# First experts: one expert ahead in two banks, or two and four ahead in three

## The reference

```python
logits = x @ router_weight.T
topw, topi = jax.lax.top_k(jax.nn.softmax(logits, axis=-1), 8)
topw = topw / jnp.sum(topw, axis=-1, keepdims=True)
...
gu = jnp.einsum('ech,ehf->ecf', xe, gate_up_proj)   # 64 experts, 128 rows, 256 -> 192
g, u = jnp.split(gu, 2, axis=-1)
h = jax.nn.silu(g) * u
ye = jnp.einsum('eci,eih->ech', h, down_proj)       # 96 -> 256
```

## Time and profile before

| | us |
|---|---|
| median of 3 timed runs | 817.23 (816.66 to 817.79) |
| span of the profiled execution | 851.6 |
| TensorE busy in it | 786.6 (92%) |
| VectorE, ScalarE, GpSimd busy | 556.9, 394.8, 271.2 |
| the expert stage, first to last down product | 433.4 to 547.6 |

### The profile page before, as it was taken

The page is one execution under the profiler, slowest core; times in us unless marked ns, Lnnn a source line. Parts: engine busy times, 40 slices in busy tenths (PEclk is TensorE's granted clock), DMA queues, the critical chain, the costliest instruction groups (busy, mean ns, idle before and its releaser), DMA issues.

```text
span 851.6 us, 16159 instructions
## 1 busy us (share of the span) xinstructions
PE 786.6 (92%) x4635; PEld 660.7 (78%) x4635; DVE 556.9 (65%) x1423; ACT 394.8 (46%) x898; POOL 271.2 (32%) x357
## 2 busy tenths in 40 slices
PE   8998999999899999999879998899999799999957
PEld 7887877778787887777677877788897688888746
DVE  4324778877778787777345555468856387778536
ACT  1334656656565666655123343323333266666411
POOL 2004445534333232222345545524415100000241
PEclk9999999999999999999889999999999999999979
DMA  7449950000000000073176999687621335555321
GB/s 212 102 107 384 406 198 34 34 27 27 21 27 28 20 21 14 27 240 135 51 230 184 323 319 296 213 288 257 246 99 69 106 112 150 149 149 153 95 69 49
DMA packets 62881, 120.74 MB, mean 142 GB/s; under 512 B 18272, under 2 KB 32864, under 8 KB 62688
## 3 DMA queue, kind: packets, MB, share of 16 engines
q1 hardware_dynamic: 51824, 95.41, 35.2%
q0 software_dynamic: 7680, 21.51, 7.0%
q10 hardware_dynamic: 3312, 3.02, 1.0%
HBM read 76.13 MB, written 43.78 MB: 141 GB/s over the span
## 4 chain that ended last, share of the span: by engine, by line
PE 65%; DVE 11%; issue 11%; ACT 4%; POOL 3%; another core or an unknown queue 3%; DMA 2%; DVEq 0%; SPq 0%; ACTq 0%; POOLq 0%
PE scores L1627 9%; PE scores L1625 8%; PE scores L1626 8%; PE scores L1849 5%; PE acc_ps L2035 4%; PE misc_ps L1755 3%; PE probsT_ps L1762 3%; PE probsT_ps L1740 3%; PE misc_ps L1753 3%; DVE xT_lo L1096 3%; PE scores L1859 3%; PE acc_ps L1740 2%; PE probsT_ps L1979 2%; DVE neg_max L1090 2%
## 5 line engine op out<-in xcount | busy, mean ns | idle before, releaser
L826 ACT ACTIVATE area<-scores,neg_max 128x128 f32<-128x128 f32 (+7 forms) x128 | 94.9, 742 | 87.7 <-DVE neg_max L1090 85.5
L1090 DVE TENSOR_REDUCE neg_max<-scores 128x1 f32<-128x128 f32 (+7 forms) x128 | 95.8, 750 | 22.1 <-PE scores L1712 20.8
L708 POOL DMA_INDIRECT xe_d<-x_rows,send_i x64 | 64.1, 1001 | 55.5 <-ACT x_rows L850 38.5
L738 POOL DMA_INDIRECT ye_d<-area,home_i x64 | 61.4, 959 | 58.7 <-issue 28.6
L1849 PE MATMUL scores<-area 128*96 128x128 f32 x512 | 69.1, 279 | 2.1 <-issue 1.3
L1625 PE MATMUL scores<-kT_hi,weff_hi 128*128 128x512 f32 (+3 forms) x172 | 66.8, 388 | 0.9 <-ACT area L803 0.4
L1849 PEld LDWEIGHTS scores<-area 128*96 128x96 f32 x512 | 60.5, 166 | 5.2 <-issue 2.7
L1627 PE MATMUL scores<-kT_hi,weff_lo 128*128 128x512 f32 (+3 forms) x172 | 61.7, 359 | 0.0
L1626 PE MATMUL scores<-kT_lo,weff_hi 128*128 128x512 f32 (+3 forms) x172 | 61.5, 358 | 0.0
L696 POOL CAST weff_hi<-area 128x256 fp32r<-128x256 f32 x42 | 17.0, 406 | 136.5 <-PE scores L1712 88.8
L1755 PE MATMUL misc_ps<-xT_lo,xT_hi 128*128 128x512 f32 x144 | 58.4, 406 | 2.2 <-DVE xT_lo L1096 2.1
(11 more groups left out here) (290 smaller groups left out, 2081.4 us busy)
## 6 DMA issues: line engine op xcount, KB each, us to landing
area<-w SPq DMA_DIRECT2D x23, 512.0 KB, 4.0
area<-gate_up SPq DMA_DIRECT2D x24, 384.0 KB
xe_d<-area SPq DMA_DIRECT2D x8, 1088.0 KB, 11.3
ye_d<-area SPq DMA_DIRECT2D x8, 1024.0 KB, 16.7
area<-w SPq DMA_DIRECT2D x8, 1024.0 KB, 7.2
area<-ye_d SPq DMA_DIRECT2D x15, 512.0 KB, 5.2
area<-xe_d SPq DMA_DIRECT2D x28, 272.0 KB
area<-down SPq DMA_DIRECT2D x24, 192.0 KB
```

The lines of the kernel that those rows point to most:

```text
L826: act.activation(row_of(n)[:, 0:L], score_bank(n)[:, 0:L], ACT.Exp, bias=neg_max[:, n % 4:n % 4 + 1], accum_out=rsum[:, s, k:k + 1]).then_ ...
L1090: dve.tensor_reduce(neg_max[:, n % 4:n % 4 + 1], score_bank(n)[:, 0:(n // HEADS + 1) * P], AX.X, ALU.max, negate=True).then_inc(max_ready, 1)
```

## The change

The buffers `xeT`, `sg` and `hT` become three deep. The banks behind T are now `pT[0]`, `pT[1]` and `acc`, those behind G are `half[0]`, `half[1]` and `misc`; the two banks behind D and the rings of eight stay. TensorE's list becomes T(e+4), G(e+2), D(e), after a start of T(0), T(1), G(0), T(2), G(1), T(3). ScalarE's becomes silu(e+2), out(e); VectorE's copy(e+4), product(e+2), homes as before. The silu waits in addition for the product that has read its buffer three experts ago. Behind the loop TensorE waits for the last product before it writes to `misc`.

```diff
+DEEP = 3
...
-        xeT = cutB3(2, HC, P)
-        sg = cutB3(2, P)[0:I0]
-        hT = cutB3(2, P)[0:I0]
+        xeT = cutB3(DEEP, HC, P)
+        sg = cutB3(DEEP, P)[0:I0]
+        hT = cutB3(DEEP, P)[0:I0]
...
+        rows_ps, gated_ps = [pT[0], pT[1], acc], [half[0], half[1], misc]
...
-            def expert_act(e, u):
-                b = u % 2
+            def expert_act(e):
+                b = e % DEEP
                 act.wait_ge(gu_ready, e + 1)
-                act.activation(sg[:, b, :], half[b][0:I0, 0:P], ACT.Silu).then_inc(silu_done, 1)
+                if past(e, DEEP):
+                    act.wait_ge(h_done, e + 1 - DEEP)
+                act.activation(sg[:, b, :], gated_ps[b][0:I0, 0:P], ACT.Silu).then_inc(silu_done, 1)
...
             for e in range(E0):
+                if e + 4 < E0:
+                    copy_xeT(e + 4)
                 if e + 2 < E0:
-                    copy_xeT(e + 2, (e + 2) % RING)
-                if e + 1 < E0:
-                    gated(e + 1, (e + 1) % RING)
+                    gated(e + 2)
...
             transpose_rows(0, 0)
             transpose_rows(1, 1)
-            gate_up(0, 0)
+            gate_up(0)
+            transpose_rows(2, 2)
+            gate_up(1)
+            transpose_rows(3, 3)
             for e in range(E0):
+                if e + 4 < E0:
+                    transpose_rows(e + 4, (e + 4) % RING)
                 if e + 2 < E0:
-                    transpose_rows(e + 2, (e + 2) % RING)
-                if e + 1 < E0:
-                    gate_up(e + 1, (e + 1) % RING)
-                down(e, e % RING)
+                    gate_up(e + 2)
+                down(e)
...
             pe.wait_ge(ye_done, E0)
+            pe.wait_ge(h_done, E0)
             run_idle(8)
```

More of the change, by code:

```diff
@@ L881, in expert_out @@
                 act.activation(ye[:, u, :], half[2 + u % 2][:, 0:HID], ACT.Copy, scale=hw[:, 0, u:u + 1]).then_inc(ye_done, 1)
-            expert_act(0, 0)
+            expert_act(0)
+            expert_act(1)
             for e in range(E0):
-                if e + 1 < E0:
-                    expert_act(e + 1, (e + 1) % RING)
+                if e + 2 < E0:
+                    expert_act(e + 2)
                 expert_out(e, e % RING)
@@ L1256, in _, with copy_xeT, gated @@
             dve.reciprocal(wsum[:], wsum[:]).then_inc(winv_done, 1)
-            def copy_xeT(e, u):
+            def copy_xeT(e):
+                b = e % DEEP
                 dve.wait_ge(xeT_ps, e + 1)
[L1260 to L1264, removed]
+                if past(e, DEEP):
+                    dve.wait_ge(gu_ready, e + 1 - DEEP)
+                dve.tensor_copy(xeT[:, b], rows_ps[b][:, 0:HID].rearrange("p (c n) -> p c n", c=HC)).then_inc(xeT_done, 1)
+            def gated(e):
+                b = e % DEEP
                 dve.wait_ge(silu_done, e + 1)
-                if past(e, 2):
-                    dve.wait_ge(ye_ps, e - 1)
-                dve.tensor_tensor(hT[:, u % 2, :], sg[:, u % 2, :], half[u % 2][0:I0, P:2 * P], ALU.mult).then_inc(h_done, 1)
+                if past(e, DEEP):
+                    dve.wait_ge(ye_ps, e + 1 - DEEP)
+                dve.tensor_tensor(hT[:, b, :], sg[:, b, :], gated_ps[b][0:I0, P:2 * P], ALU.mult).then_inc(h_done, 1)
             def find_mine(e, u):
@@ L1299, in _ @@
             dve.wait_ge(homes_made, 2)
-            copy_xeT(0, 0)
-            copy_xeT(1, 1)
+            copy_xeT(0)
+            copy_xeT(1)
             find_mine(0, 0)
             find_home(0, 0)
-            gated(0, 0)
+            copy_xeT(2)
+            gated(0)
+            copy_xeT(3)
+            gated(1)
             for e in range(E0):
+                if e + 4 < E0:
+                    copy_xeT(e + 4)
                 if e + 2 < E0:
-                    copy_xeT(e + 2, (e + 2) % RING)
-                if e + 1 < E0:
-                    gated(e + 1, (e + 1) % RING)
+                    gated(e + 2)
                 if e % 2 == 0 and e + 2 < E0:
@@ L1834, in transpose_rows, with gate_up @@
                     pe.wait_ge(ld_xe[u // 2], turn(e, u))
-                if past(e, 2):
-                    pe.wait_ge(xeT_done, e - 1)
+                if past(e, DEEP):
+                    pe.wait_ge(xeT_done, e + 1 - DEEP)
                 for c in range(HC):
-                    last = pe.transpose(pT[u % 2][:, c * P:(c + 1) * P], xe[:, u, c * P:(c + 1) * P], ident[:])
+                    last = pe.transpose(rows_ps[e % DEEP][:, c * P:(c + 1) * P], xe[:, u, c * P:(c + 1) * P], ident[:])
                 last.then_inc(xeT_ps, 1)
-            def gate_up(e, u):
-                b = u % 2
+            def gate_up(e):
+                b = e % DEEP
                 pe.wait_ge(xeT_done, e + 1)
                 await_weights(pe, e)
-                if past(e, 2):
-                    pe.wait_ge(h_done, e - 1)
+                if past(e, DEEP):
+                    pe.wait_ge(h_done, e + 1 - DEEP)
                 for part in range(2):
                     for c in range(HC):
-                        last = pe.matmul(half[b][0:I0, part * P:(part + 1) * P],
+                        last = pe.matmul(gated_ps[b][0:I0, part * P:(part + 1) * P],
                                          weights_of(e)[0][:, c, part * I0:(part + 1) * I0], xeT[:, b, c, :],
@@ L1852, in gate_up, with down @@
                 last.then_inc(gu_ready, 1)
-            def down(e, u):
-                b = u % 2
+            def down(e):
                 pe.wait_ge(h_done, e + 1)
@@ L1858, in down @@
                     pe.wait_ge(ye_done, e - 1)
-                pe.matmul(half[2 + b][:, 0:HID], hT[:, b, :], weights_of(e)[1], start=True, stop=True).then_inc(ye_ps, 1)
+                pe.matmul(half[2 + e % 2][:, 0:HID], hT[:, e % DEEP, :], weights_of(e)[1], start=True, stop=True).then_inc(ye_ps, 1)
             transpose_rows(0, 0)
             transpose_rows(1, 1)
-            gate_up(0, 0)
+            gate_up(0)
+            transpose_rows(2, 2)
+            gate_up(1)
+            transpose_rows(3, 3)
             for e in range(E0):
+                if e + 4 < E0:
+                    transpose_rows(e + 4, (e + 4) % RING)
                 if e + 2 < E0:
-                    transpose_rows(e + 2, (e + 2) % RING)
-                if e + 1 < E0:
-                    gate_up(e + 1, (e + 1) % RING)
-                down(e, e % RING)
+                    gate_up(e + 2)
+                down(e)
             def transpose_x2(t, u):
```

## The result

The changed kernel takes 822.22 us (median of 4 runs, 821.84 to 823.48) against 817.51 for the kernel before in the same session (4 runs, 816.66 to 817.83). The ratio is 1.0076, with a 95% interval of 1.0049 to 1.0104: slower, by 4.7 us by the medians and 6.2 by the ratio. That lies inside the range (811.0 to 823.0), on the side forecast, but at about two to two and a half times the forecast +2.5, in the band of rival C (821.5 to 824).

The account below looks back on a forecast made before the run. TensorE, busy 786.6 of 851.6 us, was taken as the bound. Slack 0, Start +0.9, End +0.8 and Prefetch +0.8 sum to +2.5 us, from 817.23 to 819.7 us; range 811.0 to 823.0.

Parts of the forecast that it names:

- rival C: Expert stage: loads share a nearly full DMA, TensorE waits for rows at every even transposition; 821.5 to 824 us, chance 0.13.
- Slack: Expert stage: one pitch more to hide late signals, worth 0 to -14.7 us; taken as 0, signals assumed punctual.
- rival A: Expert stage: late signals are in the timed runs too and the change hides them; 810 or 814 us, chance 0.35.
- The recorded span: Whole profiled execution: late signals hidden in part, so its span shrinks by some 7 us while timed runs do not.
- Start: First experts: the first down product stands behind more transpositions whose rows arrive one by one; net +0.9 us.
- End: Last experts: the last three down products come bunched and their sends queue on POOL; +0.8 us, bounds 0 and 1.3.
- Prefetch: Middle of the expert stage: row loads get 4.8 us to land instead of 7.9; +0.8 us taken.
- The upper bound of the step: Row loads in mid-stage: if landing takes 5.2 us, pitches become 1.59 us, +2.6 us over 40 experts.
- The sentence on DMA bandwidth: Expert stage: a 1.53 us pitch needs 369 GB/s where rows show 305 at share 0.95, against any faster pitch.
- Weights have 6.0 us and are less tight: Expert stage: weight loads keep 6.0 us before use, so they are less tight than the row loads.

Follow-up runs that it names:

- B2: The kernel before, unchanged, recorded a second time: 814.0 us (one run), span 811.9 us.
- T+4 G+1: The changed kernel with gate and up products only one expert ahead of the down product, transposition still four ahead: 820.89 us (one run).

## Why the prediction was right or wrong

**Direction: right**, and by the parts named: TensorE runs at its pitch of 1.53 us in B2 already, so working further ahead has nothing to hide, and start, end and prefetch each cost something. Only their sizes were open.

***Slack*, 0: right, with a wrong reason beside it.** The inference from 851.6 against 817.23, that most late signals belong to the execution that was recorded, holds: there is none in any other trace. But I had weighed the rule of the Trainium skill ("NOTIFIC — the notification-queue block", section 7.1, Overflow), that the block's internal pipeline always holds its producers back rather than lose a record, as something that would make signals late only while recording. The timed runs are recorded as well, and in the 13 later traces signals are punctual: recording alone doesn't do it. What disturbed that one execution stays open. This decides against rival A too (0.35): with punctual signals the repeated gap on TensorE, which the Trainium skill ("Perfetto Trace Analysis", Identifying Performance Opportunities) says can mean too few buffers, isn't there.

**The recorded span: wrong.** "The recorded span should shrink by some 7 us, while the timed runs do not" had the late signals in every record. The record after had none and is 31.6 us shorter than the disturbed one. The sum for the timed runs did not rest on it. The lesson is that a span 34 us above the median is a reason to distrust the record itself, not recording.

***Start*, +0.9: +1.3 in the traces.** Built as forecast: D(0) behind T(4), 2.7 us later, and 1.34 of it in hand. Rows arrive some 1.2 to 1.4 us apart; B2's order makes its long wait for row 5 (until 430.36) and the changed one for row 6 (until 431.56), one row later.

***End*, +0.8: +0.85.** The last three sends are 1.26 apart, as written, and undoing the order there undoes it.

***Prefetch*, +0.8: this is the step that failed, by its size.** The mechanism, T waiting for rows whose lead was cut, is in the trace (7.1 us of waits from 445 to 525 where B2 has 0.3). The term measured +3.9 us against B2 and +1.1 against the trace with three banks in the old order. By the timings it is 2.5 (0.76% less the 0.46% that stay without later weights; the two intervals together allow -0.6 to 5.5), and 2.4 by the other way round (0.56% over the three banks in the old order, 4.6 us, less 1.3 and 0.85 for start and end). So it is some three times the forecast by the timings, and its size is less well known than its cause.

The step gave 272 KB 4.8 us to land and asked whether landing is 3.9 or 5.2. It is 4.8 in the median of the changed kernel, exactly the point from which C was said to decide, and 5.6 where the stall is (473.50 to 479.1 above). Both bounds came from loads elsewhere in the kernel, and I chose near the lower one. The 4.8 us allowed are a little long too: in the earlier trace rows T stands 0.44 us behind D and not 0.65, which leaves 4.6, and the shortest leads measured are 4.7. A median landing that equals the lead is late half of the time; a stall isn't repaid, since TensorE has no spare time behind it. The upper bound of the step, +2.6 us over 40 experts, stopped at 5.2 and lies under the 3.9. Nor is one landing time the right form of the step: with B2's 6.6 the same sum gives (1.95 + 6.6 + 7.2) / 9 = 1.75 us a pitch, +8.8 over 40 experts, far too much: in the changed kernel the landing was no longer 6.6.

The sentence on DMA bandwidth had the cause in hand: with the share at 0.91 and 0.96 in B2's windows there is little left to catch up with. It should have moved the chance from the forecast to C. But its figures don't hold: 369 GB/s for a pitch of 1.53 us is more than B2 moves at that very pitch (326 at a share of 0.94 from 466 to 530), which is also above the 321 taken for a full share. The step's other half, "Weights have 6.0 us and are less tight", is wrong too: the 6.0 is right, but at 6.1 the kernel before stalled for 4.7 us, and wherever a stalled G's landings are known it had waited for the down weights, by the count that they share with gate and up.

**What stays open.** The stalls are read from one trace per kernel. The timings show the sum (+0.76%) and that it takes the order and not the banks; that a part goes with the weight loads is in the traces, and the timings only agree with it. They show no single term. Of the pair without later weights the timed difference (0.46%, 3.7 us) is more than the 2.3 us between its traces. A longer ring and T+3 with G+1 in SyncE's old order (by the leads some 6.1 us for rows, 7.5 for weights) weren't tried, nor was a semaphore of their own for the down weights. Why the rows' landing differs between 4.8 and 6.6 us is open.

## What to carry to other kernels

More run-ahead on the consumer's side shortens the lead of whatever is prefetched into a fixed ring. Count the pitches from the release of a slot to the first use, before and after, and compare them with the spread of landing times in that stage (for the rows 2.7 to 9.5 us here, with medians from 4.0 to 6.6), not with one figure from elsewhere. Do it for each kind of load: here 5 us were too few for rows and 6 too few for weights, and curing one showed the other. Look at what a wait counts: a product that waits for a sum of two loads waits for the later one, whether it uses it or not. Before a record is taken to pieces, compare its span with the timed runs; if it is several per cent longer, look for another record.

## What the runs showed of the hardware

Much of the spread between runs of one kernel goes with the clock: over 23 runs of the kernel before in the first session, time and mean granted clock correlate at -0.86. Single stretches of 3.4, 6.8 or 10.2 us fall to half clock, at places that recur (about 77, 537 and 615 us) but not in every run; one trace, T+4 G+1, has one inside the stage, from 427.0. One in the changed kernel, in the windows:

```profile
612.00:616.00 4.00, 4.00 (x37) 3.92 (x36) 2.37 (x5) 2.23 (x5) 0.00 (x0) 1.00 0.77 267
616.00:619.40 3.40, 3.40 (x14) 3.01 (x15) 3.02 (x31) 0.21 (x1) 0.00 (x0) 0.56 0.74 302
```

A grant of 0.56 is the 1.2 GHz level for nearly all of the 3.4 us; in the 4 us from 612 to 616 the clock was full (1.00) and TensorE as busy. TensorE isn't as busy ahead of every fall: ahead of the fall at 532.7 us in the run with the homes earlier TensorE was busy 5.76 of 8.70 us. B2 has no such stretch between 85 and 810 us, and the three banks in the old order have none ahead of 811; these two are the shortest records here (811.9 and 811.6 us, clock 0.998 and 1.000). The changed kernel's has 0.992. The run with the homes earlier shows both in one kernel: 818.06 us at a clock of 0.998 and 822.46 at 0.990. So up to 1.7 us of the +2.1 behind the last send, half of the 3.4 above, is this and not the change (an estimate from these rows), and a part of any difference between two single runs is too.
